# A four-layer network on one core: the second convolution's read-back moved in the sync queue, and the last layer's routing, buffers and bias rearranged

## The reference

```python
def cond(x, embedding, ...):              # layers 0, 2 and 3
    h = gelu(gelu(embedding @ W0 + b0) @ W1 + b1)
    att = softmax(h @ W2 + b2)            # 8 kernels
    return einsum('boi,bih->boh', einsum('bk,koi->boi', att, weight), x) + (att @ bias_k)[:, :, None]
# layer 1: a grouped convolution (9 taps) instead, plus c @ c_weight.T and a bias
# layer 0 ffn: (silu(x @ W_gate.T) * (x @ W_up.T)) @ W_down.T
# layer 1 ffn: x @ W_base.T + b_base + top-2 routed low-rank product of 8 experts
# layer 2 ffn: flat * w_sum + w_dense @ expert_bias, softmax over 64 experts, top 8
def layer3_ffn(x, weight, bias, gate_w, in_channel_scale, out_channel_scale):
    routing = softmax(x @ gate_w.T)       # 8 experts
    in_scale, out_scale = routing @ in_channel_scale, routing @ out_channel_scale
    return (x * in_scale) @ sign(weight).T * out_scale + bias
x = x + ffn_l(cond_l(x))                  # l = 0, 1, 2, 3
```

## Time and profile before

| | |
|---|---|
| median of 3 runs | 581.22 us (581.1 to 581.5) |
| the profiled execution | 581.92 us, its span 579.9 us |
| mean granted clock of TensorE | 0.983 |
| TensorE busy (matmul) | 549.5 us (95%) |
| TensorE busy (weight load) | 421.6 us (73%) |
| VectorE busy | 263.1 us (45%) |
| GpSimd busy | 186.7 us (32%) |
| ScalarE busy | 134.1 us (23%) |
| chain that ended last | TensorE 82%, VectorE 9%, DMA 4% |

### The profile page before, as it was taken

The page is one execution under the profiler, slowest core; times in us unless marked ns, Lnnn a source line. Parts: engine busy times, 40 slices in busy tenths (PEclk is TensorE's granted clock), DMA queues, the critical chain, the costliest instruction groups (busy, mean ns, idle before and its releaser), DMA issues.

```text
span 579.9 us, 7213 instructions
## 1 busy us (share of the span) xinstructions
PE 549.5 (95%) x2689; PEld 421.6 (73%) x2689; DVE 263.1 (45%) x529; ACT 134.1 (23%) x230; POOL 186.7 (32%) x152
## 2 busy tenths in 40 slices
PE   7999999999999999999999998699999999886996
PEld 5788888888888888888888863254455889764774
DVE  4542254522227222245222264435262687767775
ACT  4322223222223222232222221101010132232232
POOL 2699981200002100012000008600000155466986
PEclk9999999999999999999999999699999999997999
DMA  9398230490000400003050059494910343110412
GB/s 303 134 419 312 50 93 0 107 176 24 0 0 32 131 0 0 0 0 92 1 128 1 0 193 172 65 144 57 178 18 1 90 114 86 19 18 1 139 62 109
DMA packets 84211, 50.32 MB, mean 87 GB/s; under 512 B 69600, under 2 KB 74464, under 8 KB 83424
## 3 DMA queue, kind: packets, MB, share of 16 engines
q1 hardware_dynamic: 82096, 38.97, 30.8%
q0 software_dynamic: 2016, 11.01, 5.3%
q10 hardware_dynamic: 80, 0.08, 0.0%
HBM read 31.93 MB, written 8.62 MB: 70 GB/s over the span
## 4 chain that ended last, share of the span: by engine, by line
PE 82%; DVE 9%; DMA 4%; SPq 2%; issue 2%; POOL 1%; ACT 1%; DVEq 0%; POOLq 0%
PE ps L529 80%; DMA xs<-in_x 2%; SPq L308 2%; DVE cT L940 1%; DVE rcat L1167 1%; DMA stg<-y_dram 1%; POOL x_all L483 1%; DVE rest L1122 1%; DVE x_all L940 1%; DMA y_dram<-prod 1%; PE ps L769 1%; DVE lg L940 1%; DVE c_lo L940 0%; DVE ex L940 0%; DVE t L940 0%
## 5 line engine op out<-in xcount | busy, mean ns | idle before, releaser
L529 PE MATMUL ps<-c_lo,wl 128*128 128x512 f32 x448 | 172.9, 390 | 0.4 <-POOL c_lo L408 0.3
L529 PE MATMUL ps<-c_hi,wl 128*128 128x512 f32 x448 | 173.1, 390 | 0.2
L940 DVE TENSOR_TENSOR hff<-silu,ps 128x512 f32<-128x512 f32 x56 | 38.5, 688 | 163.2 <-PE ps L529 163.1
L529 PEld LDWEIGHTS ps<-c_lo,wl 128*128 128x128 f32 x448 | 84.1, 188 | 18.6 <-POOL c_lo L408 0.7
L529 PEld LDWEIGHTS ps<-c_hi,wl 128*128 128x128 f32 x448 | 84.1, 188 | 18.1 <-ACT c_hi L830 0.8
L529 PE MATMUL ps<-wl,h_hi 128*128 128x512 f32 x224 | 87.7, 391 | 0.0
L529 PE MATMUL ps<-wl,h_lo 128*128 128x512 f32 x224 | 87.2, 389 | 0.0
L940 DVE TENSOR_TENSOR h_lo<-hff,h_hi 128x512 fp32r<-128x512 f32 x56 | 46.1, 823 | 39.1 <-ACT h_hi L830 39.1
L408 POOL TENSOR_TENSOR c_lo<-cT,c_hi 128x512 fp32r<-128x512 f32 x8 | 10.7, 1343 | 158.1 <-ACT c_hi L830 158.1
L830 ACT ACTIVATE h_hi<-hff 128x512 fp32r<-128x512 f32 x56 | 35.4, 632 | 112.5 <-DVE hff L940 112.5
L864 ACT ACTIVATE silu<-ps 128x512 f32<-128x512 f32 x56 | 33.5, 598 | 116.4 <-PE ps L529 116.4
(11 more groups left out here) (155 smaller groups left out, 651.5 us busy)
## 6 DMA issues: line engine op xcount, KB each, us to landing
wl<-in_wl POOLq DMA_DIRECT2D x14, 768.0 KB, 10.0
stg<-y_dram SPq DMA_DIRECT2D x64, 128.0 KB, 4.9
xs<-in_x SPq DMA_DIRECT2D x4, 1024.0 KB, 7.9
x_all<-in_x SPq DMA_DIRECT2D x1, 4096.0 KB, 14.5
y_dram<-prod SPq DMA_DIRECT2D x16, 256.0 KB, 2.3
xs<-x_all SPq DMA_DIRECT2D x4, 1024.0 KB, 4.9
out_x<-x_all SPq DMA_DIRECT2D x16, 256.0 KB, 2.0
bias_bc<-bias_dram SPq DMA_DIRECT2D x15, 256.0 KB, 5.0
```

Source lines behind the costliest of these rows:

```text
L529: return pe.matmul(o, l, r, start=start, stop=stop)
L940: return dve.tensor_tensor(o, a, b, op)
```

## The change

In the sync program `regroup(1)` and `bias(1, 1)` now stand right behind the ten loads of `s_weights1`, ahead of the wait for the last up product, of the eight loads of `s_weights23` and of `put_back(3)`. The loop behind covers groups 2 and 3.

In the last layer:

- the block-diagonal weights have a second buffer (in `prod`) for odd groups, and those of group 1 are built before the last four `add_scaled`;
- the mixed input has a second buffer (`xs`) for odd groups, `cT3(g)`;
- exponentials and shares of the routing stand in PSUM bank 4 instead of `ex`;
- all four mixing chunks of group 1 come ahead of the first routing turn, in banks 6, 7, 2, 3, and their additions right behind the first `route3`;
- the input scales of group 0 go to banks 4 to 7 like those of the others;
- the bias is added tile by tile, group 0's before `split_x(0)`, and group g + 2's behind the finish of group g.

```diff
+        blk_odd = prod[:].rearrange("p j k o -> p (j k o)")[:, 0:TOK].rearrange("p (j n) -> p j n", j=GT)
+        def blk_of(l, g):
+            return blk_odd if l == 3 and g % 2 else blk
+        exps3, shares3 = [bank(4)[:, n * P:n * P + GT * E3].rearrange("p (j e) -> p j e", e=E3) for n in (2, 3)]
+        def cT3(g):
+            return xs if g % 2 else cT
-        IN_BANKS0, EARLY, LATE = [4, 5, 2, 3], (2, 3), (0, 1)
+        FIRST3 = ((2, 6), (3, 7), (0, 2), (1, 3))
...
                 sp.dma_start(dst[:], A[src]).then_inc(s_weights1, 16)
+            regroup(1)
+            bias(1, 1)
             sp.wait_ge(s_up, G * M)
...
             put_back(G - 1)
-            for g in range(1, G):
+            for g in range(2, G):
                 regroup(g)
                 bias(1, g)
...
-                if not isinstance(g, int) or g > 0:
+                if l == 3 and g > 0:
+                    if g > 1:
+                        pool.wait_ge(s_cond_mm[l], (g - 1) * S)
+                elif not isinstance(g, int) or g > 0:
                     pool.wait_ge(s_cond_mm[l], g * S)
...
             block_diagonal(3, 0)
+            block_diagonal(3, 1)
             add_scaled(G - 1)
...
-                xg = x_all[:, g * GT:(g + 1) * GT, :]
-                pool.tensor_tensor(xg, xg, bias3[:].unsqueeze(1).broadcast_to([P, GT, D]), ALU.add).then_inc(s_bias3, 1)
+                for j in range(g * GT, (g + 1) * GT):
+                    pool.tensor_tensor(x_all[:, j, :], x_all[:, j, :], bias3[:], ALU.add).then_inc(s_bias3, 1)
...
-            block_diagonal(3, 1)
+            bias_3(0)
+            block_diagonal(3, 2)
             split_x(0)
-            bias_3(0)
+            bias_3(1)
+            block_diagonal(3, 3)
             for g in range(G - 1):
-                if g + 2 < G:
-                    block_diagonal(3, g + 2)
-                bias_3(g + 1)
                 finish_3(g, range(GT - 1))
                 split_x(g + 1)
                 finish_3(g, [GT - 1])
+                if g + 2 < G:
+                    bias_3(g + 2)
...
-            cond_chunk(3, 1, EARLY[0], 4 + EARLY[0])
-            turn_logits3(0)
-            cond_chunk(3, 1, EARLY[1], 4 + EARLY[1])
+            for n, (s, b) in enumerate(FIRST3):
+                if b < 4:
+                    pe.wait_ge(s_x_new[2], GT * (G - 1) + b + 1)
+                cond_chunk(3, 1, s, b)
+                if n == 0:
+                    turn_logits3(0)
             turn_routing(0)
             in_scales(0)
-            out_scales(0, (0, 1))
-            for s in LATE:
-                pe.wait_ge(s_scaled, s + 1)
-                cond_chunk(3, 1, s, 4 + s)
-            out_scales(0, (2, 3))
+            out_scales(0)
...
-                exp(s_shifted3, s_exp3, g, E3)
+                act.wait_ge(s_shifted3, g + 1)
+                act.activation(exps3, lg[:, :, 0:E3], ACT.Exp).then_inc(s_exp3, 1)
...
-                link(dve.tensor_reduce(stat[:, 1], e, AX, ALU.add))
+                link(dve.tensor_reduce(stat[:, 1], exps3, AX, ALU.add))
                 link(dve.reciprocal(stat[:, 2], stat[:, 1]))
-                link(tt(e, e, bc(stat[:, 2], E3), ALU.mult))
+                link(tt(e, exps3, bc(stat[:, 2], E3), ALU.mult))
...
                 route3(g)
+                if g == 0:
+                    cond3(1, FIRST3)
...
                 split_x(g, 1)
-                if g == 0:
-                    cond3(1, (0, 1))
                 split_x(g, 3)
-                if g + 1 < G:
-                    cond3(g + 1, range(2 if g == 0 else 0, S))
+                if 0 < g < G - 1:
+                    cond3(g + 1, [(s, UPPER[s]) for s in range(S)])
```

More of the change, by code:

```diff
@@ L415, in block_diagonal @@
                     pool.wait_ge(s_cond_mm[{2: 0, 3: 2}[l]], G * S)
-                pool.tensor_tensor(blk[:].rearrange("p j (b o) -> p j b o", b=TB),
+                dst = blk_of(l, g)
+                pool.tensor_tensor(dst[:].rearrange("p j (b o) -> p j b o", b=TB),
                                    agg[:, COND[l], ds(g * GT, GT)].unsqueeze(2).broadcast_to([P, GT, TB, ROWS]),
@@ L495, in split_x @@
                     pool.wait_ge(s_scaled_hi, S * g + s + 1)
-                    pool.tensor_tensor(lo[:, s], cT[:, s], hi[:, s].bitcast(F32), ALU.subtract).then_inc(s_scaled_lo_even, 1)
+                    pool.tensor_tensor(lo[:, s], cT3(g)[:, s], hi[:, s].bitcast(F32), ALU.subtract).then_inc(s_scaled_lo_even, 1)
             def bias_3(g):
                 pool.wait_ge(s_cond_mm[3], S * (g + 1))
-                xg = x_all[:, g * GT:(g + 1) * GT, :]
-                pool.tensor_tensor(xg, xg, bias3[:].unsqueeze(1).broadcast_to([P, GT, D]), ALU.add).then_inc(s_bias3, 1)
+                for j in range(g * GT, (g + 1) * GT):
+                    pool.tensor_tensor(x_all[:, j, :], x_all[:, j, :], bias3[:], ALU.add).then_inc(s_bias3, 1)
             def finish_3(g, js):
-                pool.wait_ge(s_bias3, g + 1)
+                pool.wait_ge(s_bias3, GT * (g + 1))
                 for j in js:
@@ L568, in cond_chunk @@
                     x = x_all[:, g * GT + j, cols(s)] if l == 3 else xs[:, j, cols(s)]
-                    ins = mm(bank(b)[:, cols(j)], x, blk[:, j])
+                    ins = mm(bank(b)[:, cols(j)], x, blk_of(l, g)[:, j])
                 ins.then_inc(s_cond_mm[l], 1)
@@ L740, in router3 @@
                     for j in range(GT):
-                        ins = mm(bank(4)[j * QUAD:(j + 1) * QUAD, 0:P], wr3[:, s, 0:QUAD], cT[:, s, cols(j)],
+                        ins = mm(bank(4)[j * QUAD:(j + 1) * QUAD, 0:P], wr3[:, s, 0:QUAD], cT3(g)[:, s, cols(j)],
                                  s == 0, s == S - 1)
@@ L774, in in_scales @@
                 for s in range(S):
-                    mm(bank(4 + s if g else IN_BANKS0[s]), in_w[:, cols(s)], wT[:]).then_inc(s_in_scale, 1)
+                    if g == 0 and s == 2:
+                        pe.wait_ge(s_cT[3], S + 2)
+                    mm(bank(4 + s), in_w[:, cols(s)], wT[:]).then_inc(s_in_scale, 1)
             def out_scales(g, js=range(GT)):
                 for j in js:
-                    if g == 0 and j in IN_BANKS0:
-                        pe.wait_ge(s_scaled, IN_BANKS0.index(j) + 1)
+                    if g == 0 and j == 2:
+                        pe.wait_ge(s_cT[3], 2 * S)
                     if g:
@@ L921, in high @@
                     act.wait_ge(s_scaled, S * g + n + 1)
-                    copy(halves(g)[0][:, n], cT[:, n]).then_inc(s_scaled_hi, 1)
+                    copy(halves(g)[0][:, n], cT3(g)[:, n]).then_inc(s_scaled_hi, 1)
                 def out_scale(j):
@@ L1157, in route3 @@
                 lt = bank(4)[:, P:2 * P].rearrange("p (j e) -> p j e", j=GT)[:, :, 0:E3]
-                e = ex[:, :, 0:E3]
+                e = shares3
                 link(dve.tensor_reduce(stat[:, 0], lt, AX, ALU.max))
@@ L1175, in scale_in @@
                     dve.wait_ge(s_in_scale, S * g + s + 1)
-                    tt(cT[:, s], cT[:, s], bank(4 + s if g else IN_BANKS0[s]), ALU.mult).then_inc(s_scaled, 1)
+                    tt(cT3(g)[:, s], cT3(g)[:, s], bank(4 + s), ALU.mult).then_inc(s_scaled, 1)
             def split_x(g, s):
@@ L1180, in split_x @@
                 dve.wait_ge(s_scaled_hi, S * g + s + 1)
-                tt(lo[:, s], cT[:, s], hi[:, s].bitcast(F32), ALU.subtract).then_inc(s_scaled_lo_odd, 1)
+                tt(lo[:, s], cT3(g)[:, s], hi[:, s].bitcast(F32), ALU.subtract).then_inc(s_scaled_lo_odd, 1)
             def scale_out(g, js):
@@ L1191, in cond3 @@
                 dve.wait_ge(s_bias_bc[3], 16 * (g + 1))
-                for s in chunks:
-                    n = (EARLY + LATE).index(s) if g == 1 else s
+                for n, (s, b) in enumerate(chunks):
                     dve.wait_ge(s_cond_mm[3], S * g + n + 1)
-                    dve.wait_ge(s_scaled_lo_odd if s % 2 else s_scaled_lo_even, 2 * (g - 1) + s // 2 + 1)
-                    tt(cT[:, s], bank(4 + s), bias_bc[:], ALU.add).then_inc(s_cT[3], 1)
+                    tt(cT3(g)[:, s], bank(b), bias_bc[:], ALU.add).then_inc(s_cT[3], 1)
             for g in range(G):
@@ L1209, in _ @@
                 split_x(g, 1)
-                if g == 0:
-                    cond3(1, (0, 1))
                 split_x(g, 3)
-                if g + 1 < G:
-                    cond3(g + 1, range(2 if g == 0 else 0, S))
+                if 0 < g < G - 1:
+                    cond3(g + 1, [(s, UPPER[s]) for s in range(S)])
             scale_out(G - 1, range(GT))
-            dve.wait_ge(s_bias3, G)
+            dve.wait_ge(s_bias3, NT)
             dve.wait_ge(s_rescaled, NT)
```

## The result

The changed kernel takes 589.04 us (median of 4 runs, 586.66 to 590.75) against 581.16 for the kernel before in the same comparison: a ratio of 1.0149, 95% interval 1.0091 to 1.0206. It is slower, as forecast, but by more: +7.9 us where the forecast was +2.5. The profiled execution took 588.53 us, its span 586.3.

What follows compares the result with a forecast made beforehand. TensorE, busy 95% of the span, bounds the kernel; time is won only where it idles or runs at lower clock. +12.1 - 9.6 = +2.5 us on the 581.2 median: 583.7 us, own range 581 to 587, whole range 574.5 to 590.5.

Steps and rivals of the forecast that it cites:

- Part 1: Second layer: read-back of group 1 moved up the sync queue; in all +12.1 us, bounds +3 and +18.
- Rival 3: Second layer: the read-back, not the exponential, was the gate; 561.8 us, chance 0.05.
- L: Landing of the eight weight loads that ScalarE waits for: 364.5, the middle of bounds 362.4 and 366.8.
- Rival 2: Loads land at 362.4 and the chain to `hm` slips past GpSimd's bias addition; 574.7 to 576.7 us, chance 0.24.
- The chain: Layer 1, exponential to `hm`: meets GpSimd's bias addition, so TensorE goes on at 375.0, 7.7 us later.
- The additions: VectorE's two pairs after the second convolution meet GpSimd's bias additions: TensorE 3.1 us later, plus 1.3 of clock.
- rival 1: VectorE loses its turn between two additions to GpSimd's waiting operation; TensorE idles 7.4 us, 589.3 us, chance 0.16.
- Part 2: Last layer: routing chain in PSUM, second buffers, early chunks, bias by tiles; gains 9.6 us, bounds 4 and 10.5.
- the clock 2.7: Last layer, group 1's routing turn to next router: 10.1 us at clock 1.00 instead of 12.8 at 0.77.
- the later turns: Last layer: later routing chains met single-tile additions, costing TensorE 1.05 and 0.32 us idle; both go, 1.4 us.
- the tail: End of the kernel after the last layer's routing turns: claimed unchanged.
- Rival 4: Last layer: the routing chain in PSUM waits as before, gain only 4 us; 589.3 us, chance 0.08.

## Why the prediction was right or wrong

**Part 1, the gate: right.** The sum's main step was that the wait for the read-back goes and the exponential, queued behind eight loads, takes its place. The changed kernel shows it (17.41 us, released by `hm`), and moving the exponential alone takes it away again. Rival 3, that the read-back was the gate, is dead.

**L, 364.5 by the prediction, 366.5 in the trace: too early by 2.** I took the middle of two bounds and the upper one, 366.8, was right: the first load's issue takes 3.37 us, so it waits for the read-back ahead of it. The read-back's own issue took 11.90 us where I had 10.7; it landed at 356.6 as forecast (356.4). The Trainium skill's page "DMA: Bandwidth & Descriptors", section "Queues, rings and completion order", says that each DMA engine consumes its descriptors in ring order. The trace agrees: the first load landed 5.7 us after its issue, at 358.4 and behind the read-back, where it took 2.6 from an empty queue, and all eight were in 9.9 us after the read-back, 13.8 after their first issue, where they took 10.35. Rival 2 needed L at its low end and the chain past GpSimd's bias addition, and neither was so.

**The chain: the sum right, by luck.** It met the bias addition as forecast and `hm` ended at 376.9, L + 10.4, where the working had L + 10.45. So TensorE went on at 377.05 for 375.0: +9.7 us instead of +7.7, all of it L. But two errors cancel in it. The bias addition ended at 373.14, L + 6.6, and not at L + 8.05. And from its end to that of `hm` it took 3.8 us and not 2.4: the copy `t<-m` had waited for the bias addition (1.20 us), so more of the chain was left, and in it the addition `stat<-m` took 0.71 us and a `TENSOR_SCALAR` 0.90 beside GpSimd's small differences. Each of the three takes 0.17 in the next group.

**The additions: the step that failed.** I gave VectorE both additions of a pair between two GpSimd operations and put "loses its turn" into rival 1 at a chance of 0.16. It does lose it. The first pair and the first two bias operations, one by one:

```profile
377.68 4.51 POOL L477 TENSOR_TENSOR x_all<-x_all,bbase 128x2048 f32 x1 [0.37 <-POOL out_w L489]
...
381.41 1.33 DVE L961 TENSOR_TENSOR cT<-tr,bias_bc 128x512 f32<-128x512 f32 x1
...
382.15 4.97 POOL L477 TENSOR_TENSOR x_all<-x_all,bbase 128x2048 f32 x1
...
382.67 5.01 DVE L961 TENSOR_TENSOR cT<-tr,bias_bc 128x512 f32<-128x512 f32 x1
```

They end in turn: bias operation 382.19, addition 382.74, bias operation 387.12, addition 387.68. The pair in the run with the loads first and the pairs against single tiles show the same step at two other lengths. The idle stretch was 5.45 us instead of 3.1, and it did drop the clock: 1.55 us in the router where I had taken 1.3. Together +7.1 instead of +4.4.

Rival 1 had 7.4 us of idle. It was less because the bias operations began 0.6 us behind the convolution's start and not 2.1 as in the working, so the second pair met the last of them with none queued behind it. With the operations at these places and both additions of a pair in one turn, I estimate from the same rows an idle stretch of 1.4 us. So the lost turn cost about 4 us, more than the 2.4 between 5.45 and 3.1.

Rival 1's total, 589.3, is close to the measured 589.04, in part by luck: its terms are +17.7 - 9.6 = +8.1, measured in the spans are +16.8 - 10.4 = +6.4. Likeliest was the wrong case of the two, and 589.04 lies outside the forecast's own 581 to 587; the whole range, 574.5 to 590.5, held it.

**Part 2: right, a little small.** 9.6 forecast, 10.4 between the traces, 9.8 by the ratio of that part alone. By steps: up to the turn of group 1, 5.5 forecast, 0.7 + 5.3 = 6.0 measured; the clock 2.7 and 2.6 (12.75 less 10.13); the later turns 1.4 and 1.6; the tail 0 and 0.1. What I undersized is the first group's start, whose four chunks and additions hardly delayed the scaling. Rival 4, a PSUM chain that waits as before, is dead (casts of 0.29 us beside the bias tiles). Its bound of 577 us for a chain that waits for single tiles was close to 578.06 for just that kernel.

**The sum.** +16.8 - 10.4 instead of +12.1 - 9.6. The error of 4 us in the span is 2.0 in L and 2.7 in the additions and their clock, less 0.8 in part 2. Another 1.5 us of the +7.9 between the medians isn't in the spans of the two profiled executions (6.4) and lies inside the scatter of the changed kernel's runs, 586.7 to 590.8.

## What to carry to other kernels

Before a transfer is moved ahead in a queue, list what stands behind it there, and for each of those who waits for it and what that engine has queued behind its wait: here a load for layers 2 and 3 gated an exponential of layer 1 by the mere order of ScalarE's program. Where a wait in an engine's program guards work that isn't urgent, put the urgent instruction ahead of it. Split long GpSimd operations where VectorE works on two SBUF inputs beside them, and keep short dependent chains in PSUM. A loss and a gain in one change are worth taking apart: one half won 1.7%, the other lost 3.2%, and together with the mended order of the loads and the bias by tiles that other gave 1.2%.

## What the runs showed of the hardware that was not expected

Take two VectorE additions in a row, both with two SBUF inputs, while GpSimd operations are queued without a gap. The first waits for the end of the GpSimd operation under way, and the second for one whole operation more. A pair took 6.26 us against operations of 4.5 us and 2.65 to 3.42 us against operations of 1.2 us, for 1.25 us when GpSimd is idle. The starts and ends show the order in which they finish; the trace doesn't show who holds what.

Tiny operations lose their turn too. In the run with the exponential first, group 1's chain on VectorE fell among GpSimd's three bias operations:

```profile
377.11 13.45 POOL L477 TENSOR_TENSOR x_all<-x_all,bbase 128x2048 f32 x3 [0.37 <-POOL out_w L489]
...
377.48 4.16 DVE L965 TENSOR_TENSOR stat<-m 128x4 f32<-128x4 f32 x1
381.67 4.46 DVE L965 TENSOR_TENSOR lg<-ex,rest 128x32 f32<-128x32 f32 x1
...
386.39 4.21 DVE L1116 TENSOR_SCALAR stat<-stat 128x4 f32<-128x4 f32 x1
```

Each ends with one of GpSimd's three operations; undisturbed they take 0.17 to 0.19 us. It cost that run only 0.41 us of TensorE's time, because a base product of 15.41 us ran beside the chain.

A VectorE copy of 128x8 elements from SBUF to SBUF (`t<-m`) took 1.20 us beside a GpSimd addition and takes 0.17 in the next group, where GpSimd is idle, so it waited to that addition's end at 373.14. Like the `TENSOR_SCALAR` it has one SBUF input only; the prediction's working named the additions alone.
